# Attention and channel mixing on eight cores: a row sum moved from ScalarE to VectorE, and a residual addition moved from VectorE to GpSimd

## The reference

```python
def attn(x, Wq, Wk, Wv):            # on layernorm(x)
    q = x @ Wq; k = x @ Wk; v = x @ Wv
    att = jnp.einsum('bid,bkd->bik', q, k)
    att = jax.nn.softmax(att, axis=1)
    return jnp.tile(jnp.matmul(att, v), (1, 1, 16))

def ffn(x, W_r, W_k, W_v, mu_r, mu_k):   # on layernorm(x)
    x_prev = shift of x by one token, zero ahead of the first
    r = sigmoid((mu_r * x + (1 - mu_r) * x_prev) @ W_r.T)
    k = (mu_k * x + (1 - mu_k) * x_prev) @ W_k.T
    return r * (square(relu(k)) @ W_v.T)

x = x + attn(layernorm(x))
x = x + ffn(layernorm(x))
```

## Time and profile before

| what | us |
|---|---|
| median of 2 runs | 746.9 (745.93 to 747.88) |
| profiled execution, its own time | 751.89 |
| its span (slowest core, core 5) | 750.3 |
| spans of the 8 cores | 735.1 to 750.3 |
| busy in the span: PE, DVE, ACT, POOL | 355.2, 308.7, 243.9, 47.7 |

### The profile page before, as it was taken

The page is one execution under the profiler, slowest core; times in us unless marked ns, Lnnn a source line. Parts: engine busy times, 40 slices in busy tenths (PEclk is TensorE's granted clock), DMA queues, the critical chain, the costliest instruction groups (busy, mean ns, idle before and its releaser), DMA issues.

```text
span 750.3 us, 5723 instructions; the slowest of 8 cores (735.1 to 750.3 us)
## 1 busy us (share of the span) xinstructions
PE 355.2 (47%) x1392; PEld 124.1 (17%) x1392; DVE 308.7 (41%) x531; ACT 243.9 (33%) x420; POOL 47.7 (6%) x77
## 2 busy tenths in 40 slices
PE   0004000005967887777761000000226999999884
PEld 0001000002421111111111000000002443444331
DVE  3702607147721111111130687726991001226887
ACT  3104014050028898888840332200002324330000
POOL 2201102011000030000000011000000000001110
PEclk9999555556985556666655555555577999999998
DMA  9955975856310099900000014494200000005784
GB/s 230 298 115 104 296 119 181 216 112 119 50 30 8 7 132 164 273 6 0 1 0 1 4 36 160 166 179 92 43 0 0 1 1 0 1 1 212 240 260 186
DMA packets 76996, 75.82 MB, mean 101 GB/s; under 512 B 59427, under 2 KB 59443, under 8 KB 76900
## 3 DMA queue, kind: packets, MB, share of 16 engines
q0 software_dynamic: 13504, 32.32, 16.6%
q1 hardware_dynamic: 12516, 30.49, 13.0%
q10 hardware_dynamic: 50944, 12.65, 11.1%
HBM read 47.79 MB, written 21.56 MB: 92 GB/s over the span
## 4 chain that ended last, share of the span: by engine, by line
DMA 33%; PE 23%; DVE 20%; issue 10%; ACTq 7%; ACT 5%; DVEq 1%; POOL 0%; SPq 0%; POOLq 0%
DMA v_sb<-vdram 14%; PE ktp L909 7%; PE rps L869 7%; DMA zdram<-zst 6%; ACTq L335 5%; DMA xst<-x_in 4%; DMA z1T<-z1dram 3%; DMA y_out<-x2b 3%; ACT p_sb L577 3%; DVE x1b L708 3%; DVE xk L848 3%; PE dpool L517 3%; DVE zst L376 2%; ACTq L799 2%; DVE sums L388 2%
## 5 line engine op out<-in xcount | busy, mean ns | idle before, releaser
L577 ACT ACTIVATE p_sb<-dpool,negm 128x1024 bf16<-128x1024 f32 x128 | 140.5, 1123 | 21.9 <-DVE negm L542 20.5
L869 PE MATMUL rps<-wrT,xr 128*128 128x512 bf16 x256 | 59.7, 399 | 161.6 <-DVE xr L839 141.4
L517 PE MATMUL dpool<-qrep,krep 64*128 64x512 bf16 x256 | 101.9, 566 | 41.5 <-ACT p_sb L577 37.1
L416 PE MATMUL qk<-zT,wqk 128*128 128x512 bf16 x64 | 18.5, 441 | 167.9 <-DVE qrep L447 101.4
L321 ACT ACTIVATE zst<-xst 128x1024 bf16<-128x1024 f32 x32 | 33.8, 1057 | 108.6 <-issue 96.4
L966 PE MATMUL ops<-wvT,kaT 128*128 128x512 bf16 x256 | 57.2, 379 | 6.9 <-DVE tmp L1011 5.4
L548 DVE TENSOR_REDUCE ell<-ellp 128x1 f32<-128x4 f32 x32 | 5.0, 157 | 134.6 <-ACT p_sb L577 134.6
L869 PEld LDWEIGHTS rps<-wrT,xr 128*128 128x128 bf16 x256 | 25.9, 102 | 194.9 <-issue 167.5
L909 PE MATMUL ktp<-xk,wkT 128*128 128x512 bf16 x256 | 55.6, 379 | 1.7 <-ACT r_sb L882 1.3
L934 DVE TENSOR_TENSOR kaT<-kaT 128x512 bf16<-128x512 bf16 x32 | 13.6, 426 | 98.5 <-ACT kaT L925 98.5
L388 DVE TENSOR_REDUCE sums<-xst 128x1 f32<-128x1024 f32 x32 | 37.1, 1216 | 10.0 <-DMA xst<-x_in 10.0
(11 more groups left out here) (83 smaller groups left out, 386.7 us busy)
## 6 DMA issues: line engine op xcount, KB each, us to landing
xst<-x_in SPq DMA_DIRECT2D x32, 512.0 KB, 10.4
xst<-x_in POOLq DMA_DIRECT2D x32, 512.0 KB, 6.4
zdram<-zst POOLq DMA_DIRECT2D x32, 256.0 KB, 10.2
y_out<-x2b SPq DMA_DIRECT2D x16, 512.0 KB, 3.3
z1dram<-z1b SPq DMA_DIRECT2D x16, 256.0 KB, 4.5
wrT<-wrT_in POOLq DMA_DIRECT2D x1, 2048.0 KB, 19.1
wkT<-wkT_in POOLq DMA_DIRECT2D x1, 2048.0 KB, 31.6
wvT<-wvT_in POOLq DMA_DIRECT2D x1, 2048.0 KB, 44.0
```

The source lines that it names most:

```text
L416: t.matmul(qk[buf][:, :], wqk[:, ct * 128:(ct + 1) * 128], zT[ct][:, nch * 512:(nch + 1) * 512], start=(ct == 0), stop=(ct == CT - 1), ski ...
L517: t.matmul(units[u][:, cc * 512:(cc + 1) * 512], krep[64 * a:64 * (a + 1), kt * 128:(kt + 1) * 128], qrep[64 * a:64 * (a + 1), c * 512:(c ...
L577: sc.activation(p_sb[kt % 4][:, s * 1024:(s + 1) * 1024], units[u][:, :], AF.Exp, bias=negm[:, kt:kt + 1], accum_out=ellp[:, 4 * (kt % 2) + s:
L869: ins = t.matmul(r_ps[t_ % 2][:, hh * 512:(hh + 1) * 512], xr[ct][:, t_ * 128:(t_ + 1) * 128], wrT[:, ct * C + hh * 512:ct * C + (hh + 1) ...
```

## The change

In the attention stage the exps of the even tile of a pair no longer use the accumulator; DVE instead sums the tile's 4096 bf16 values in `p_sb`. The odd tile is as before. In the output stage POOL waits for each of its loads, adds `out_tok` to the loaded x in place, and signals SH; DVE's own addition of `out_tok` goes, and its last addition waits for SH instead of for the load.

```diff
-        k_tmp = lambda t: SV_K0 + 3 * t + 1
-        k_mid = lambda t: SV_K0 + 3 * t + 2
-        k_x2 = lambda t: SV_K0 + 3 * t + 3
+        k_tmp = lambda t: SV_K0 + 2 * t + 1
+        k_x2 = lambda t: SV_K0 + 2 * t + 2
...
                     v.wait_ge(SS, d_exp(kt, 3))
-                    v.reduce_sum(ell[:, kt:kt + 1],
-                                 ellp[:, 4 * (kt % 2):4 * (kt % 2) + 4],
-                                 axis=AX.X).then_inc(SV, 1)
+                    if kt % 2 == 0:
+                        v.reduce_sum(ell[:, kt:kt + 1],
+                                     p_sb[kt % 4][:, :],
+                                     axis=AX.X).then_inc(SV, 1)
+                    else:
+                        v.reduce_sum(ell[:, kt:kt + 1],
+                                     ellp[:, 4:8],
+                                     axis=AX.X).then_inc(SV, 1)
...
-                        sc.activation(p_sb[kt % 4][:, s * 1024:(s + 1) * 1024],
-                                      units[u][:, :], AF.Exp,
-                                      bias=negm[:, kt:kt + 1],
-                                      accum_out=ellp[:, 4 * (kt % 2) + s:
-                                                     4 * (kt % 2) + s + 1]).then_inc(SS, 1)
+                        if kt % 2 == 0:
+                            sc.activation(p_sb[kt % 4][:, s * 1024:(s + 1) * 1024],
+                                          units[u][:, :], AF.Exp,
+                                          bias=negm[:, kt:kt + 1]).then_inc(SS, 1)
+                        else:
+                            sc.activation(p_sb[kt % 4][:, s * 1024:(s + 1) * 1024],
+                                          units[u][:, :], AF.Exp,
+                                          bias=negm[:, kt:kt + 1],
+                                          accum_out=ellp[:, 4 + s:
+                                                         4 + s + 1]).then_inc(SS, 1)
...
                 g.dma_start(out=xst[:, (t_ % 8) * C:(t_ % 8 + 1) * C],
                             in_=x_in[t_ * 128:(t_ + 1) * 128, :]).then_inc(FSs[t_ % 8], 16)
+                g.wait_ge(FSs[t_ % 8], fs_k(t_))
+                g.tensor_tensor(xst[:, (t_ % 8) * C:(t_ % 8 + 1) * C],
+                                xst[:, (t_ % 8) * C:(t_ % 8 + 1) * C],
+                                bass.AP(out_tok, t_ * D, [[TOWN * D, 128], [0, 16], [1, D]]),
+                                ALU.add).then_inc(SH, 1)
...
+                v.wait_ge(SH, t_ + 1)
                 v.wait_ge(SV, k_tmp(t_))
-                v.tensor_tensor(tmp32[:, (t_ % 2) * C:(t_ % 2 + 1) * C],
-                                tmp32[:, (t_ % 2) * C:(t_ % 2 + 1) * C],
-                                bass.AP(out_tok, t_ * D, [[TOWN * D, 128], [0, 16], [1, D]]),
-                                ALU.add).then_inc(SV, 1)
-                v.wait_ge(FSs[t_ % 8], fs_k(t_))
-                v.wait_ge(SV, k_mid(t_))
                 v.tensor_tensor(x2b[:, (t_ % 2) * C:(t_ % 2 + 1) * C],
                                 tmp32[:, (t_ % 2) * C:(t_ % 2 + 1) * C],
                                 xst[:, (t_ % 8) * C:(t_ % 8 + 1) * C], ALU.add).then_inc(SV, 1)
```

## The result

The changed kernel takes 840.35 us (median of 11 runs, 837.83 to 846.36), the kernel before 748.91 (median of 10, 745.08 to 754.85); the ratio is 1.1223, with a 95% interval of 1.1183 to 1.1264. So it is 91 us slower. 845 us were forecast, with a range of 814 to 868. Here and in the experiments, executions that fell into a second, slower state of the chip are left out of the ratios, but not of the medians.

A forecast was written before the change was run, and what follows sets the result against it. No one item was taken to lead: ACT and serial DVE work bound attention, DVE's pace the output stage. 746.9 us plus 56.5 (attention) and 42 (output) gave 845 us, with a range of 814 to 868.

The forecast's parts named there:

- The reduce: Attention stage: each of 16 DVE sums over 4096 bf16 takes 4.41 us, with a lower bound of 2.28.
- the double pace of bf16: Attention stage, a rival: the bf16 sum runs at twice the float pace, 2.28 us, giving 811 us; chance 0.10.
- Its place: Attention stage: the even sum stands on ACT's path at each border between passes, 4.06 us more a pass.
- What ACT saves: Attention stage: exps without accumulator reads save 0.15 us each, so DVE's sum starts 0.53 us earlier a pass.
- POOL's chain: Output stage: landing 4.7, 0.1 and addition 2.04 us follow serially, 6.84 us a tile, +42 us (bounds +13 to +72).
- No contention here: Output stage: DVE's x2b falls into POOL's wait for the next load, not into POOL's addition.
- the third rival: Output stage: POOL's addition is held up by x2b, slower, or clock falls; 8 us a tile, 865 us and up; chance 0.09.
- the upper bound of 3.3 us: Output stage: POOL's addition at most 3.3 us, its 2.04 plus one DVE addition that holds it up.
- The clock: PE's clock may fall to its lower level: no cost in the attention stage, 5 us at most in the output stage.
- Nothing in between: Between the attention and output stages, 390 to 676 us, no length changes.
- The sum: Whole kernel: attention +56.5 and output +42 us, together +98.5 on a base of 746.9.

The follow-up runs named there:

- the kernel with negm first: Attention half of the change alone, but DVE computes both negm of the next pass before this pass's sums; 745.5 us, 0.9938 of the kernel before.
- The run with loads ahead: Output half of the change alone, but POOL issues each load four tiles ahead of its addition; 757.9 us, 1.0214 of the kernel before.

## Why the prediction was right, step by step

- **The reduce**: 4.41 us worked out, 4.42 measured. The choice between 1x and the double pace of bf16 was the largest open term, 34 us, and the row of the same operation decided it rightly.
- **Its place**: +4.06 us a pass from the sum's start to ACT; the rows give 6.42-2.45 = 3.97. That it is the place and not the work is shown by the kernel with negm first.
- **What ACT saves**: taken as 0.15 us an exp and 0.53 a pass, measured 0.08 to 0.09 and 0.36. This term was over-sized by half: the middle between the bounds had no better reason than being the middle, and the value is near the end that the row of L882 gave. The stage came to +58.2 instead of +56.5. In the last pass the delay stands where it was put: PE waits 4.6 us for the last scaled tile.
- **POOL's chain**: the mechanism is as told, including what is queued behind the waiting addition; the wait group of 16 with 63.6 us is it. The two sizes were off in opposite directions: landing 4.0 instead of 4.7 (the discount from the crowded median of 5.3 was too small), addition 2.34 instead of 2.04 (the ratio of two memsets was too low). Turn 6.45 instead of 6.84, stage +36 instead of +42 on the cores shown. A third error lies in the base: the 4.09 us a tile of the kernel before are those of the core with the shortest output stage; its eight cores have 4.09 to 4.46, and over eight cores the stage is +31.7. So this term was over-sized by 10 us, a third.
- **No contention here**: what was said against the third rival held, `x2b` stayed at 1.22 us because it falls into POOL's wait. The run with loads ahead shows that this hangs on the schedule: once nobody waits, the two collide. Then it is DVE that is held up, and not POOL's addition, as the rival and the upper bound of 3.3 us had it.
- **The clock**: 0.89 in the output stage's stretch instead of 0.96, and 0.62 in a pass, both without a cost that the waits show: in the output stage PE waits 28.2 us for DVE's `tmp`, in the attention stage 85.8 us for ACT's exps.
- **Nothing in between**: right, -2.4 us on the cores shown and +1.3 over eight, with cores of one kernel up to 7 us apart.
- **The sum**: +98.5 forecast, +91.4 measured. The forecast of 845 is closer to 840.35 than that, 4.7 us, since the base of 746.9 was the median of two runs and that of ten is 748.9. That part is luck.

## What to carry to other kernels

Work moved to an idle engine costs by its place in that engine's order: ask who is queued behind it and what they hold up. The same 70 us of sums cost 58 us, nothing, 50 us or 8 us, by where the neighbours stood (each with the reads that they spare ACT). A load, its wait and its consumer on one in-order queue make a chain of latencies; issue loads some tiles ahead of the wait. Before additions of POOL run beside DVE's, look at DVE's instructions with two SBUF inputs: here one input in PSUM took them from 3.36 us back to 1.23. And read a stretch on all cores before it is called a gain or a loss: the one core shown was off by 4.5 us here.

## What the runs showed of the hardware that was not expected

- A DVE addition with both inputs in SBUF was held up under four POOL additions in a row, 12.45 us in place of 1.23, though it was issued at 678.30 us, ahead of the first of them (678.66), while POOL was issuing a load, and though between the additions POOL did nothing but issue loads. It got through only when POOL waited for something else. At the end of the stage it happened again, 10.23 us under four more. It isn't the issuing of loads that holds it: in the changed kernel an `x2b` addition at 753.08 us took 1.22 beside a load issue at 752.86. POOL's own additions were never longer than 2.37 us in this run. So here not the earlier instruction won, but POOL; POOL's recorded starts may be rough to some tenths of a us, but the second, third and fourth of its additions started 3.2 us and more behind DVE's.
- A POOL addition of 1024 floats with one operand tiled 16 times took 2.33 to 2.38 us in every run, 1.9 times DVE's 1.23.
- An accumulator read of 0.22 us costs ACT 0.08 to 0.09, since most of it lies beside the next exp.
